# A 16-batch attention and ffn sandwich on one core: batch 0 transposed by TensorE, its scores begun on half the keys, and the calls ahead of the loop reordered

## The reference

```python
def attn(t):                       # t: (16, 1024, 256)
    qkv = einsum('bnd,ed->bne', t, W_qkv) + b_qkv
    Q, K, V = qkv[:, :, :256], qkv[:, :, 256:512], qkv[:, :, 512:]
    scores = einsum('bqd,bkd->bqk', Q, K) / sqrt(256)
    return einsum('bqk,bkv->bqv', softmax(scores), V)
def ffn(x):                        # hidden 768, integer weights / 127
    return einsum('bsh,dh->bsd', silu(x @ wg.T) * (x @ wu.T), wd)
x = x + layernorm(attn(layernorm(x)))
x = x + layernorm(ffn(layernorm(x)))
```

## Time and profile before

| | us |
|---|---|
| median of 3 runs | 1371.56 (1370.83 to 1371.71) |
| the profiled execution, its own time | 1371.36 |
| its span, first to last instruction | 1369.5 |
| time outside the span | 1.86 |
| PE busy in the span | 1348.6 |

### The profile page before, as it was taken

The page is one execution under the profiler, slowest core; times in us unless marked ns, Lnnn a source line. Parts: engine busy times, 40 slices in busy tenths (PEclk is TensorE's granted clock), DMA queues, the critical chain, the costliest instruction groups (busy, mean ns, idle before and its releaser), DMA issues.

```text
span 1369.5 us, 22379 instructions
## 1 busy us (share of the span) xinstructions
PE 1348.6 (98%) x7406; PEld 725.4 (53%) x7406; DVE 902.2 (66%) x2167; ACT 875.3 (64%) x1371; POOL 828.0 (60%) x1007
## 2 busy tenths in 40 slices
PE   8989999999999999999999999999999999999997
PEld 4445455554555555555554555545555555555554
DVE  7886565766766666666766657567666666656555
ACT  5667576666757577475766766567575774756644
POOL 4677384664837648475583846648376483745545
PEclk9999999999999999999999999999999999999999
DMA  8995482845638366382654737456382663716411
GB/s 211 200 181 131 78 155 78 137 110 104 135 89 155 73 130 140 70 169 72 121 132 78 154 80 137 108 101 138 87 155 76 123 138 78 139 55 119 90 40 56
DMA packets 437192, 158.29 MB, mean 116 GB/s; under 512 B 418129, under 2 KB 420433, under 8 KB 437074
## 3 DMA queue, kind: packets, MB, share of 16 engines
q1 hardware_dynamic: 436272, 156.03, 55.2%
q10 hardware_dynamic: 802, 0.79, 0.2%
HBM read 36.70 MB, written 16.78 MB: 39 GB/s over the span
## 4 chain that ended last, share of the span: by engine, by line
PE 88%; DVE 4%; SPq 2%; DMA 2%; issue 2%; POOL 2%; ACT 1%; ACTq 0%; POOLq 0%; DVEq 0%
PE S L765 88%; SPq L256 1%; DMA yTl<-yl 1%; DVE S L697 1%; DVE mxs L668 1%; DVE st L706 1%; POOL rs L305 0%; DVE st L650 0%; SPq L237 0%; POOL Pl L356 0%; POOL yl L383 0%; DMA xs<-in_L_attn_t 0%; SPq L262 0%; DVE st L724 0%; DVE X L719 0%
## 5 line engine op out<-in xcount | busy, mean ns | idle before, releaser
L466 ACT ACTIVATE P<-S,nmx,sc 128x1024 f32<-128x1024 f32 x128 | 153.7, 1201 | 282.1 <-DVE nmx L672 282.1
L734 DVE SCALAR_TENSOR_TENSOR hf<-S,sc,hf 128x512 f32<-128x512 f32 x192 | 141.9, 746 | 140.8 <-ACT hf L501 135.0
L668 DVE TENSOR_REDUCE mxs<-S 128x1 f32<-128x1024 f32 x128 | 156.0, 1219 | 118.3 <-PE S L765 118.3
L356 POOL TENSOR_TENSOR Pl<-P,Ph 128x1024 f16<-128x1024 f32 x96 | 204.6, 2132 | 35.4 <-issue 25.7
L765 PE MATMUL S<-xTh,zTh 128*128 128x512 f16 x512 | 194.1, 379 | 4.7 <-ACT P L466 2.2
L765 PE MATMUL S<-PTh,xh 128*128 128x512 f16 x512 | 194.1, 379 | 1.0 <-DVE hf L734 1.0
L765 PE MATMUL S<-xTl,zTh 128*128 128x512 f16 x512 | 194.0, 379 | 0.0
L765 PE MATMUL S<-PTl,xh 128*128 128x512 f16 x512 | 194.0, 379 | 0.0
L765 PE MATMUL S<-PTh,xl 128*128 128x512 f16 x512 | 194.0, 379 | 0.0
L765 PE MATMUL S<-xTh,zTl 128*128 128x512 f16 x512 | 193.6, 379 | 0.0
L301 POOL TENSOR_SCALAR rs<-mv,sc 128x2 f32<-128x2 f32 (+1 forms) x96 | 35.5, 370 | 231.4 <-DVE mv L710 191.7
(11 more groups left out here) (138 smaller groups left out, 2472.4 us busy)
## 6 DMA issues: line engine op xcount, KB each, us to landing
xs<-in_L_attn_t SPq DMA_DIRECT2D x32, 512.0 KB, 5.3
X<-in_L_attn_t SPq DMA_DIRECT2D x32, 512.0 KB, 4.5
out_x<-X SPq DMA_DIRECT2D x64, 256.0 KB, 2.9
PTh<-Ph SPq DMA_TRANSPOSE x128, 3.3
PTl<-Pl SPq DMA_TRANSPOSE x128, 3.3
hTl<-in_L_ffn_w_gate SPq DMA_DIRECT2D x1, 768.0 KB, 8.1
hTh<-in_L_ffn_w_up SPq DMA_DIRECT2D x1, 768.0 KB, 9.7
hTl<-in_L_ffn_w_down SPq DMA_DIRECT2D x1, 768.0 KB, 11.0
```

Of the source, the lines that this page charges most:

```text
L356: p.engine.tensor_tensor(out=Pl[:, m % 3, :], in0=P[:, m % 2, :], in1=Ph[:, m % 3, :], op=ALU.subtract).then_inc(pl_vector if i in PL_ON_V ...
L466: a.engine.activation(P[:, m % 2, :], ps[:, bank:bank + 2, :].rearrange("p a n -> p (a n)"), ACT.Exp, bias=nmx[:, c:c + 1], scale=sS, accu ...
L668: v.engine.tensor_reduce(mxs[:, c:c + 1], ps[:, bank:bank + 2, :].rearrange("p a n -> p (a n)"), axis=AX.X, op=ALU.max, negate=True).then_ ...
L734: v.engine.scalar_tensor_tensor(out=hf[:, n % 3, :], in0=ps[:, bank + 1, :], scalar=sc2[:, 4:5], in1=hf[:, n % 3, :], op0=ALU.mult, op1=AL ...
```

## The change

Batch 0's x no longer goes through `turn_x`. ACT (tiles 0, 1, 2, 3, 6, 7) and DVE (4, 5) write x-hat in float32 to `X[2]`, `X[3]`; PE transposes it into PSUM; ACT copies out the high part, DVE the low one. `xh` and `xl` of batch 0 are still made (ACT, POOL), for `attend`. The first load is cut into three. The scores of query tiles 0 and 1 begin on the left four key tiles before the second half's z is made. V's scale joins the ffn's `turn_max` and `powers`. All lists ahead of the loop change their order; the loop and the end do not.

```diff
+X0_ON_SCALAR = (0, 1, 2, 3, 6, 7)
+X0_ON_VECTOR = (4, 5)
+XN_ON_POOL = ((1, 1), (2, 1))
...
+        def load_first(s, part):
+            ts = slice(2 * part, 2 * part + 2)
+            s.engine.dma_start(xs[:, ts, :], x_d[0, :, :].rearrange("(p t) d -> p t d", t=NT)[:, ts, :]).then_inc(x0_in[part], 16)
+
         def load_x(s, b, g):
-            xl_wait(s, b - 1, g)
+            if b == 1:
+                x0_wait(s, 4 * g + 3)
+            else:
+                xl_wait(s, b - 1, g)
...
+        def x_first_scalar(a, *tiles):
+            a.wait_ge(nb1_done, tiles[-1] // 4 + 1)
+            for t in tiles:
+                a.engine.activation(x_hat_first(t), xs[:, t, :], ACT.Identity, bias=nb1[:, t:t + 1], scale=rs1[:, t:t + 1]
+                                    ).then_inc(x0_scalar, 1)
+
+        def xT_first_high(a, g, bank, di):
+            a.wait_ge(x0_turned, 2 * g + di + 1)
+            a.engine.activation(xTh[0][:, 4 * g:4 * g + 4, di, :], cols(ps[:, bank + di, :]), ACT.Copy).then_inc(xTh0_done, 1)
...
+        def x_first_vector(v, *tiles):
+            v.wait_ge(nb1_done, tiles[-1] // 4 + 1)
...
+        def xT_first_low(v, g, bank, di):
+            v.wait_ge(x0_turned, 2 * g + di + 1)
+            v.wait_ge(xTh0_done, 2 * g + di + 1)
...
+        def x_first_turn(t, g, bank):
+            for tile in range(4 * g, 4 * g + 4):
+                x0_wait(t, tile)
+                for di in range(2):
+                    c = (tile % 4) * 128
+                    done = t.engine.transpose(ps[:, bank + di, c:c + 128], x_hat_first(tile)[:, di * 128:(di + 1) * 128],
+                                              ident[:, :])
...
+        def first_z(t, g, bank, *chosen):
+            if g:
+                t.wait_ge(zw_done, 2)
...
+        def first_scores_left(t, banks):
+            t.wait_ge(cb_ready, 1)
+            for dj in range(2):
+                t.wait_ge(zh_done, dj + 1)
...
         @block.sync
-            load_x(s, 0, 0)
             load_x(s, 0, 1)
-            turn_x(s, 0, 0, 0)
-            turn_x(s, 0, 0, 1)
-            turn_x(s, 0, 1, 0)
-            turn_x(s, 0, 1, 1)
+            load_first(s, 0)
+            load_x(s, 1, 1)
+            load_ffn(s, 1)
+            load_ffn(s, 0)
             load_x(s, 1, 0)
...
+            turn_p(s, 0, 1, 0)
             turn_p(s, 0, 0, 1)
+            turn_x(s, 1, 0, 0)
+            load_x(s, 2, 0)
+            turn_x(s, 1, 0, 1)
             turn_p(s, 0, 1, 1)
...
         @block.scalar
+            x_first_scalar(a, 0, 1, 2, 3)
+            x_first_scalar(a, 6, 7)
             A_high(a)
+            xT_first_high(a, 0, 4, 0)
+            xT_first_high(a, 0, 4, 1)
+            x_high(a, 0, 0)
+            x_high(a, 0, 1)
+            xT_first_high(a, 1, 0, 0)
+            xT_first_high(a, 1, 0, 1)
+            z_high(a, 0, 0, 2)
...
         @block.vector
+            first_stats(v, 0)
+            first_stats(v, 1)
+            first_stats(v, 2)
             copy_bq(v)
+            first_stats(v, 3)
             row_sizes(v)
+            bound(v)
             scale_A(v)
             A_low(v)
             c_scales(v)
+            x_first_vector(v, 4, 5)
+            xT_first_low(v, 0, 4, 0)
+            xT_first_low(v, 0, 4, 1)
+            xT_first_low(v, 1, 0, 0)
+            xT_first_low(v, 1, 0, 1)
+            z_float(v, 0, 0, 2)
             z_low(v, 0, 0)
-            V_low(v)
             x_stats(v, 1, 0)
+            z_float(v, 0, 1, 2)
             row_max(v, 0, 0, 4)
             x_stats(v, 1, 1)
             row_max(v, 0, 1, 6)
+            z_low(v, 0, 1)
+            V_max(v)
+            ffn_max(v, 0)
+            p_low(v, 0, 1)
             row_max(v, 0, 2, 0)
             row_max(v, 0, 3, 2)
             ffn_max(v, 1)
             ffn_max(v, 2)
...
         @block.tensor
             biases(t)
+            keep_busy(t, 19, const_done, 3, 0)
+            A_product(t)
+            sum_rows(t)
+            x_first_turn(t, 0, 4)
             c_product(t)
+            keep_busy(t, 6, const_done, 3, 0)
+            first_z(t, 0, 2, 0)
+            x_first_turn(t, 1, 0)
+            first_z(t, 0, 2, 1, 2)
+            first_scores_left(t, (4, 6))
+            first_z(t, 1, 2, 0, 1, 2)
+            first_scores_low(t, (4, 6))
+            first_scores_right(t, (4, 6))
             score(t, 0, 2, 0, None, None)
```

More of the change, by code:

```diff
@@ L430, in ffn_high @@
             a.wait_ge(ffn_in[n], 16)
+            if n == 1:
+                a.wait_ge(xl0_done, 2)
             a.engine.activation(stage[n][0], raw[n], ACT.Copy, scale=sc2[:, n:n + 1]).then_inc(w_hi, 1)
[L433 to L438, removed]
+        def x_first_scalar(a, *tiles):
[6 more added lines that the diff above has]
+            a.engine.activation(xTh[0][:, 4 * g:4 * g + 4, di, :], cols(ps[:, bank + di, :]), ACT.Copy).then_inc(xTh0_done, 1)
         def x_hat(a, b, g):
@@ L563, in bound, with powers @@
             v.wait_ge(v_step, v.tick(v_step))
[L565 to L571, removed]
+        def x_first_vector(v, *tiles):
+            v.wait_ge(nb1_done, tiles[-1] // 4 + 1)
+            for t in tiles:
+                v.engine.tensor_scalar(x_hat_first(t), xs[:, t, :], scalar1=rs1[:, t:t + 1], scalar2=nb1[:, t:t + 1],
+                                       op0=ALU.mult, op1=ALU.add).then_inc(x0_vector, 1)
+        def xT_first_low(v, g, bank, di):
+            v.wait_ge(x0_turned, 2 * g + di + 1)
+            v.wait_ge(xTh0_done, 2 * g + di + 1)
+            v.engine.scalar_tensor_tensor(out=xTl[0][:, 4 * g:4 * g + 4, di, :], in0=cols(ps[:, bank + di, :]), scalar=1.0,
+                                          in1=xTh[0][:, 4 * g:4 * g + 4, di, :], op0=ALU.mult, op1=ALU.subtract
+                                          ).then_inc(xTl0_done, 1)
+        def powers(v, c0, c1, bank, floors, turn):
             n = c1 - c0
@@ L1135, in _ @@
             x_norm(p, 0, 1)
-            x_hat_pool(p, 0, 1)
+            x_low(p, 0, 0)
+            x_low(p, 0, 1)
             x_norm(p, 1, 0)
@@ L1652, in _ @@
             row_inverse(v, 1, 0)
+            x1_add(v, 0, 0, 1)
+            o_low(v, 0, 1, 0)
             o_low(v, 0, 1, 1)
-            o_low(v, 0, 1, 0)
-            x1_add(v, 0, 0, 1)
             row_max(v, 1, 4, 0)
@@ L1659, in _ @@
             y_stats(v, 0, 1, 0)
+            p_low(v, 1, 4)
             y_stats(v, 0, 1, 1)
-            p_low(v, 1, 4)
             row_max(v, 1, 5, 2)
+            row_max(v, 1, 6, 0)
             x1_add(v, 0, 1, 0)
-            row_max(v, 1, 6, 0)
+            x1_add(v, 0, 1, 1)
             row_max(v, 1, 7, 2)
-            x1_add(v, 0, 1, 1)
             h_mul(v, 0, 0, 0, 6)
-            row_inverse(v, 1, 1)
             z_float(v, 2, 0, 0)
```

382 lines of the change are left out of this document (186 added, 196 removed).

## The result

| | before | after |
|---|---|---|
| median, us | 1371.63 (1370.83 to 1372.09, 6 runs) | 1382.17 (1380.12 to 1386.34, 6 runs) |
| the profiled execution, us | 1371.36 | 1382.01 |
| its span, us | 1369.5 | 1380.2 |
| granted TensorE clock over the span | 0.999 | 0.995 |

The changed kernel is slower: ratio 1.0079 [1.0067, 1.009], by 10.5 us. I had said 1376.0, in a range of 1368.5 to 1379.5. The side was right, the size was not: 6.2 us are missing in the sum, and the median lies outside the range. Besides, the executions now differ from each other by 6.2 us where they differed by 1.3.

What follows compares the result with a forecast made beforehand. Ahead of 50 us two engines were taken to bound: PE, and DVE's list in its order. The sum was 1371.36 + 4.7 + 0.3 - 0.4 = 1375.96, said as 1376.0 us, range 1368.5 to 1379.5.

Steps and rivals of the forecast that it cites:

- the deciding step: Batch 1's load on SP: load_x(1,0) goes behind load_x(1,1) and two ffn loads, so DVE waits 3.5 us for it.
- marks: Signs named beforehand: DVE wait on xs, PE wait on xTl, early scores, PE idle per stretch, granted clock 1.00.
- The landing of x(1,0): On SP's queue: issued after 15.35, behind 2048 KB more, x(1,0) is there at 25.25, bounds 24.0 to 27.
- The low transposition: Of x(1,0) on SP, behind load_x(2,0): 5.2 us plus 0.5 to issue the load, so project_z(1,0) at 45.9, 4.7 late.
- The powers: On DVE: the matrix comes as late as PE and V adds one step; 0.3 us more, between 0 and 1.2.
- The clock: TensorE's granted clock: forecast to stay 1.00; a fall to 1.2 GHz over the first scores had chance 0.03.
- Nothing lost later: Behind the powers: PE hardly idles from 50 to 95 us, and the 2.2 and 2.2 waits from 95 to 120 stay.
- the -0.4: Last term of the sum, 0.4 us won; the swap of x1_add and o_low could win up to 0.7.
- +4.7: First term of the sum: PE is 4.7 us late at project_z(1,0), starting at 45.9 instead of 41.20.
- Rival 1: No change: x(1,0) at 24.0, a transposition of 4.2 and 1 us less on POOL leave 1.5; 1372.9. Chance 0.24.
- rival 2: Faster: x(1,0) in by 22, score(0,4) 1.6 sooner, pw and half the 95-to-120 idling gone; 1367.1. Chance 0.19.
- Rival 3: Clock gate: 1.2 GHz over the first scores, with fewer fillers and 16 transpositions, adds 8 us; 1382. Chance 0.03.

Runs made afterwards that it cites:

- run 1: Changed kernel with load_x(1,0) moved ahead of load_x(1,1) and the two ffn loads on SP; 1378.33 us, ratio 1.0045.
- run 4: Kernel before with only SP's loads in the changed kernel's order, load_x(1,0) behind load_x(1,1) and two ffn loads; 1379.25 us, ratio 1.005.
- run 8: Changed kernel with load_x(1,0) ahead, load_x(2,0) behind turn_x(1,1), x_hat_pool(1,1) ahead of x_low(1,0), load_first(0) ahead of load_x(0,1); 1375.76 us.
- run 2: Changed kernel with load_x(2,0) moved behind the low transposition of x(1,0) on SP; 1381.07 us, ratio 1.0064.
- run 3: Changed kernel with load_x(1,0) ahead of SP's other three loads and load_x(2,0) behind the low transposition of x(1,0); 1378.53 us, ratio 1.0041.
- run 5: Changed kernel with load_x(1,0) ahead of SP's other three loads and load_x(2,0) behind both transpositions of x(1,1); 1378.17 us, ratio 1.0043.
- run 9: The kernel of run 8 with row_max(0,6) ahead of z_float(1,0) on DVE and 19 filler matmuls ahead of score(1,7); 1375.01 us, ratio 1.0023.
- run 7: Changed kernel with filler matmuls on PE ahead of score(0,4), project_z(1,0), spread_powers and score(1,7); 1380.03 us, ratio 1.0058.
- Run 12: Kernel before with z_low(0,1) ahead of p_low(0,1) on DVE, nothing else; 1371.63 us, ratio 1.0.
- the best version: The kernel of run 9 with the changed kernel's own order on POOL, x_low(1,0) ahead of x_hat_pool(1,1); 1374.54 us, ratio 1.0021.

## Why the prediction was right or wrong

The number fell outside because three parts of the way ahead of 64 us were each 1.5 to 1.8 us longer than said (x(1,0) and its transposition, the powers with the V step, the clock), and 1.1 more came behind them. None of them alone would have carried it out of the range.

**The mechanism: right.** The load order was named as the deciding step, and runs 1 and 4 show it from both sides: undone in the changed kernel it gives back 4.2 us, made alone in the kernel before it costs 7.3. Every wait I named as a mark is there: 4.95 on `xs` (said 2.5 to 5), a wait on `xTl` (2.06, said about 3), batch 1's first projection not ahead of 42. Four marks failed: PE idle from 14 to 50 us is 5.7 and not near 8 (slow matmuls count as busy), from 50 to 95 it is 1.5 and not under 1, the first score record is at 20.09 and not before 20, and the clock is not 1.00.

**The landing of x(1,0): the term mis-sized.** Said 25.25, bounds 24.0 to 27; measured 27.5. Its two parts: `load_x(1,1)` was issued at 16.75, 1.4 later than my 15.35, because the start was late; and x(1,0) took 10.8 us from there, where I had 9.9. The first has its own cause. I put tiles 0 and 1 at 5.6, with bounds 4.9 and 6.3, and they came at 7.12, outside them. I had summed bytes on one queue only, although ACT's queue had the loads of tiles 2 and 3 and of W under way from 1.28 on. Run 8, with those two tiles first on SP's queue, has them at 4.56. The Trainium skill (DMA: Bandwidth & Descriptors, Queues, rings and completion order) says that each DMA engine takes packets from its queues in turn; the 7.12 agrees with that, since by it the bytes of both queues count.

**`score(0,4)`: follows from it.** Said 33.8, came at 36.15, 2.35 later, and x(1,0) was 2.3 late.

**The low transposition: right in size.** Said 0.5 to issue the load and 5.2 from the transposition's issue, hence 45.9; it was issued at 42.95 and PE started at 47.71, 4.8. The 1.8 between forecast and measurement is again the late x(1,0), less what this step was over-priced. What I missed lies behind it: with this wait removed or shortened, nothing arrives at `attend(0,0,1)`, since `PTl`, then `pw` bind next (runs 2, 3, 5). The waits stood close behind each other, and I had treated the first as the only one.

**The powers: too low.** I took 0.3 with an upper bound of 1.2. From `project_z(1,0)` to `attend(0,0,1)` PE lost 1.8: the two further transpositions of maxima 0.2 and the wait on `PTl` 0.4, then 0.6 of additional wait on `pw` and 0.6 for the bias matmul on V that `spread_powers` now holds. I had not counted the last among PE's instructions. The added wait on `pw` is the order of DVE's list. The timeline of the changed kernel, PE, DVE and POOL:

```profile
52.99 1.03 PE L876 MATMUL S<-ident,am 128*1 128x128 f32 x8
...
53.71 1.22 DVE L719 TENSOR_REDUCE mxs<-S 128x1 f32<-128x1024 f32 x1
...
55.09 0.67 DVE L610 TENSOR_REDUCE ax<-S 1x4 f32<-1x512 f32 x1
...
55.74 2.28 POOL L364 TENSOR_TENSOR zTl<-zw,zTh 128x512 f16<-128x512 f32 x2
55.80 1.12 DVE L614 TENSOR_SCALAR ax<-ax 1x1 f32<-1x1 f32 x2
56.95 1.08 DVE L618 TENSOR_SCALAR pw<-ax 1x4 int32<-1x4 int32 x1
...
58.06 0.17 DVE L621 RECIPROCAL pw<-pw 1x4 f32<-1x4 f32 x1
```

and the same steps in the kernel before:

```profile
47.33 0.55 DVE L576 TENSOR_REDUCE ax<-S 1x3 f32<-1x384 f32 x1 [0.56 <-PE S L819]
...
47.91 1.21 DVE L579 TENSOR_SCALAR ax<-ax 1x3 f32<-1x3 f32 x1
...
49.16 1.08 DVE L581 TENSOR_SCALAR pw<-ax 1x3 int32<-1x3 int32 x1
```

Before, DVE stood ready when PE had transposed the maxima; after, they were there at 54.0 and DVE came at 55.09, behind `row_max(0,6)` (53.71). Run 9, where `row_max(0,6)` stands ahead of `z_float(1,0)`, has no wait on `pw`. The steps themselves are no longer than they were. They are long for one to four elements of one partition: each DVE group ends when one of POOL's two subtractions does (1.14 us each). The Trainium skill (SBUF — State Buffer, Who interferes with whom) says that the ports which DVE and GpSimd share go to one of them for a whole instruction; these two groups agree. The reciprocal of 0.17, at 58.06, was not held, although POOL's next subtraction had begun at 57.97. It wasn't tried with POOL idle.

**The clock: the step that failed.** I wrote "the granted clock 1.00" among the marks and gave the rival 0.03, because I looked for a dip only at the first scores, in fewer fillers. The dips came elsewhere: two of them behind waits that I had myself forecast (`score(0,4)`, the `exp` of batch 1), and the one that was paid behind the short waits on `PTl` and `pw`. The rows price that one at 1.7 us; with the fillers of run 7 the median is 2.6 us better and the spread 4.4 us smaller, not all of it by the clock; run 4 has about 3 for one wait of 7 us. A forecast of PE waits should have carried such a term. Besides, since a dip doubles what it falls on, its cost depends on whether a wait stands behind it.

**"Nothing lost later" and the -0.4.** Wrong by 1.1 in the profiled execution (0.7 lost, not 0.4 won): the waits on `exp` were kept as said (2.20), `yTl` took up most of the third dip, and `silu` held PE for 1.6 at 123 us. Why ACT reached that `silu` so late wasn't traced.

**The sum, step by step.** Forecast +4.7 + 0.3 - 0.4 = 4.6. Measured: 6.5 at `project_z(1,0)` (x(1,0) late), 1.8 instead of 0.3 to `attend(0,0,1)`, 1.7 for the dip there, 0.1 instead of -0.4 to 102 us and 0.6 behind it: 10.7.

**The rivals.** Rival 1 (no change) needed x(1,0) at 24.0, and rival 2 (faster) at 22: neither came near. Rival 3 had the time, 1382, but that is luck: it put the low clock over the first scores and 8 us on it, and those scores ran at full speed. The 16 transpositions (13.04 to 17.6) were followed by no slow matmul until 36 us, so nothing here bears out that they weaken the clock. Run 12 shows in addition that rival 2's gain of 1.6 at `score(0,4)` would have had the powers behind it: 1.2 won there became nothing.

**What stays open.** Which idle stretch of about 2 us is followed by a dip and which not; how much of the difference between executions is the start, how much the dips; and where the last 2.7 us of the best version lie. In run 8's profile, whose clock is full from 8 to 106 us, the changed order is 0.6 late at `project_z(1,0)`, 1.8 at `attend(0,0,0)` and 2.8 at `attend(0,0,1)`, so they arise at `PTl`, `pw` and the V step. No run took V's scale back out of the powers, and none put batch 0's x back on the DMA transposition, so what the transpositions on PE are worth by themselves is not shown.

## What to carry to other kernels

Where one in-order queue feeds several consumers, price the order of its loads first: moving one needed load of 512 KB behind 2 MB of others cost 7.3 us in a kernel of 1372. A wait of PE can carry a clock term of its own: here 1.7 us behind waits of 0.39 and 1.11, about 3 behind one of 7.0, nothing where another wait stood behind it, and nothing behind three waits of 1.7 to 2.2 in the kernel before. Fillers in the waits removed the dips and steadied the runs (a spread of 1.8 for 6.2, over 4 and 6 executions). And a wait removed is worth only the distance to the next one: four edits that each took 1 to 2 us of wait from PE (runs 2, 3, 5, 12) returned between nothing and 1.4 us, and the 1.4 was a dip that did not come.

## What the runs showed of the hardware

- Idle stretches of PE of 2.95 and 2.20 us, and 0.39 and 1.11 close together, were each followed by 3.4 us at 1.2 GHz; one of 7.0 by 10.2 us, 4.4 of them still within the wait. Idle stretches of 1.7, 2.2 and 1.8 us in the kernel before were followed by none. With matmuls on constants in the gaps (run 7) the clock stayed at 2.4 GHz.
- The clock column doesn't show the level at the start: with 1.00 in it, the eight float32 matmuls of `A_product` took 3.54 us in the change (0.63 for one in the median) and 1.99 in run 8 (0.38). In run 9 they took 3.67 with 0.50 in the column.
- A float32 transposition of 128x128 on PE takes 0.134 us in a row of eight (1.07 us), half of what the nearest row, a float32 128x256 product, had made me take as the upper bound, and the 1.0 that I had put for eight was near.
- The same loads at the start came in at different times in different executions: tiles 2 and 3 on ACT's queue were there at 6.5 us in run 8 and at 8.0 in run 9, with the same code up to there.
- On one partition, two ops of DVE on one element (1.12 us together) and one on four elements (1.08) ended with POOL's subtractions beside them; a reciprocal of four elements took 0.17, with POOL's next subtraction under way.
